# Layer 2's weights of a four-layer graph network from 16 concurrent 32x32 products and a table of block counts

## The reference, cut to what matters

```
def layer0(X, adj):   # mean of the neighbours, dense, relu, l2 norm
    deg = clip(sum(adj, 1) + 1, 1)
    z = concat([X, (adj @ X + X) / deg]) @ W + b
    out = relu(z); return out / max(norm(out), 1e-12)
def layer1(X, Wt=adj):
    h = tanh(concat([X, t]) @ W1 + b1)
    return h @ W2 + b2 + Wt @ (X @ B.T) - sum(Wt, 1) * (X @ B.T)
def layer2(X, adj):   # a neighbour weighs 1, 1/2, 1/4, ... from the last one of its row back
    rank = cumsum(adj != 0, 1); k = min(rank[:, -1:], 100)
    w = mask * where(pos > 0, 0.5 ** (k - pos), 0)       # pos = rank - (deg - k)
    return w @ (X @ weight) + bias
def layer3(x, adj):   # logmap(adj @ expmap(x)) @ kernel + bias
x = layernorm(x + layer_l(x))      # for l = 0, 1, 2, 3
```

## Time and profile before

| what | value |
|---|---|
| time, median of 3 runs | 167.0 us (166.5 to 167.3) |
| profiled execution | 167.19 us |
| its span | 165.3 us |
| PE busy | 123.7 us, 75% |
| DVE busy | 105.8 us, 64% |
| ACT busy | 70.6 us, 43% |
| POOL busy | 46.3 us, 28% |
| mean granted TensorE clock | 0.959 |

### The profile page before, as it was taken

One profiled execution on the slowest core, in us unless ns is written; L12 is line 12 of the kernel. 1 busy time (PEld: TensorE's weight loads), 2 busy tenths in 40 slices (PEclk: granted clock), 3 DMA queues, 4 the chain that ended last, 5 costly groups with the idle time before them and its releaser, 6 DMA issues.

```text
span 165.3 us, 2143 instructions
## 1 busy us (share of the span) xinstructions
PE 123.7 (75%) x760; PEld 67.6 (41%) x760; DVE 105.8 (64%) x235; ACT 70.6 (43%) x143; POOL 46.3 (28%) x54
## 2 busy tenths in 40 slices
PE   0000269996999999999997999989999899992000
PEld 0000159841444345346344667337447644572000
DVE  0164997999999999998961115500623888538861
ACT  0030215477567866715814576721113310257440
POOL 0000002412401241027931024400412552713290
PEclk9999999999999999999999999999999999998555
DMA  3999999999999940000000000000000000000006
GB/s 110 255 238 357 354 289 252 337 344 340 339 345 346 300 147 0 0 4 0 0 0 0 0 4 0 2 0 4 0 0 0 0 2 0 4 0 0 0 0 127
DMA packets 13946, 18.59 MB, mean 112 GB/s; under 512 B 5360, under 2 KB 5616, under 8 KB 13936
## 3 DMA queue, kind: packets, MB, share of 16 engines
q1 hardware_dynamic: 7728, 9.68, 20.6%
q10 hardware_dynamic: 6208, 8.78, 18.0%
HBM read 17.93 MB, written 0.52 MB: 112 GB/s over the span
## 4 chain that ended last, share of the span: by engine, by line
DVE 34%; PE 34%; DMA 13%; ACT 5%; POOL 4%; issue 4%; SPq 2%; POOLq 1%; DVEq 0%
PE psS L801 11%; DVE AT L556 8%; DMA stage<-adj 7%; DMA WT<-adj 7%; DVE AT L557 6%; PE psN L801 5%; PE psC L801 5%; POOL root L287 2%; PE psC L892 2%; PE psC L890 2%; POOL nroot L306 2%; DVE XP L562 2%; ACT WT L397 2%; DVE XP L561 1%; DVE u L579 1%
## 5 line engine op out<-in xcount | busy, mean ns | idle before, releaser
L397 ACT ACTIVATE WT<-psC 128x512 int16<-128x512 f32 x64 | 36.5, 597 | 13.3 <-PE psC L892 12.4
L801 PE MATMUL psS<-AT,XP 128*128 128x512 bf16 x112 | 29.9, 379 | 1.3 <-DVE XP L562 1.3
L287 POOL TENSOR_TENSOR root<-var,power 128x4 f32<-128x4 f32 (+1 forms) x16 | 18.7, 1172 | 36.5 <-DVE var L603 14.6
L892 PE MATMUL psC<-AT,cb 128*128 128x512 bf16 x64 | 24.2, 379 | 0.0
L890 PE MATMUL psC<-AT,cb 128*128 128x512 bf16 x56 | 21.4, 382 | 1.6 <-ACT WT L397 1.5
L556 DVE STREAM_TRANSPOSE AT<-stage 128x1024 bf16<-128x1024 bf16 x10 | 13.0, 1304 | 10.0 <-DMA stage<-adj 10.0
L801 PEld LDWEIGHTS psS<-AT,XP 128*128 128x128 f16 x112 | 10.4, 98 | 15.1 <-DVE XP L562 2.3
L854 PE MATMUL psH<-AT,cb 128*32 128x256 bf16 x32 | 1.7, 344 | 18.9 <-DVE AT L557 18.9
L300 POOL TENSOR_TENSOR XB<-X,weights 128x256 f32<-128x256 f32 x12 | 10.0, 843 | 18.4 <-DVE X L608 18.4
L557 DVE STREAM_TRANSPOSE AT<-stage 128x1024 bf16<-128x1024 bf16 x10 | 12.7, 1273 | 0.0
L391 ACT ACTIVATE stage<-psS 128x512 f32<-128x512 f32 x6 | 3.6, 596 | 17.6 <-PE psS L801 11.4
(11 more groups left out here) (156 smaller groups left out, 231.1 us busy)
## 6 DMA issues: line engine op xcount, KB each, us to landing
stage<-adj ACTq DMA_DIRECT2D x20, 256.0 KB, 11.3
stage<-adj SPq DMA_DIRECT2D x20, 256.0 KB, 13.4
WT<-adj ACTq DMA_DIRECT2D x12, 256.0 KB, 12.5
WT<-adj SPq DMA_DIRECT2D x12, 256.0 KB, 16.8
out<-X SPq DMA_DIRECT2D x6, 64.0 KB, 2.0
weights<-weights_packed SPq DMA_DIRECT2D x1, 353.5 KB, 17.2
X<-x SPq DMA_DIRECT2D x2, 128.0 KB, 6.8
X<-x ACTq DMA_DIRECT2D x2, 128.0 KB, 8.2
```

What stands on the lines that cost most here:

```text
L287: nc.gpsimd.tensor_tensor(root[:, e, 0:n], var[:, e, 0:n], power[:, 0:n, 0:NR], ALU.pow).then_inc(root_ready, 1)
L397: nc.scalar.activation(WT[:, e, chain_block(bank, k)], psC[bank][:], ACT.Relu).then_inc(chain_taken, 1)
L801: ins = nc.tensor.matmul(bank, XP[:, l % 2, c], matrix, start=(c == 0), stop=last)
L892: nc.tensor.matmul(acc, C("own"), AT[:, c, e], start=False, stop=True, skip_group_check=(k > 0)).then_inc(chain_ready, 1)
```

## The change

Layer 2's weights: `chain(i)` is now one step for four tiles of chunk i // 4, 16 steps in all. A step is 32 matmuls of 32x32 by 32x512: 16 from `base`, a constant, on `later`, and 16 from `own` on the matrix itself. In each set every one has its own 32 rows (q) and its own 32 columns (g) of the array; a row strip q writes its own PSUM bank. `later` is a table of counts, 17 rows per quarter, which a new matmul `spread` makes from `cnt` and ACT evicts (`take_spread`). No step needs the one before it, but the four banks of `psC` must have been evicted. ACT evicts two banks with one instruction (`take_chain(i, h)`). The tiles so made have their row quarters in another order, so layer 2's x parts are written to `ZP` and turned into that order by `turn` (16 matmuls of 128x32 per chunk, evicted by `take_turned`), before layer 2's sums.

Layer 1: two banks, `psN` and `psS`; chunks 0 and 1 first, then 2, then 3. `counts`, `spread` and `degrees` share `psX` with the transposed x and the hidden layer, from chunk 1 on. Layer 0's last chunk is counted and summed in three quarters of its columns after transposes 14, and the last quarter after transposes 15.

Other moves: centring of the weights on DVE goes from behind transposes 15 to ahead of transposes 4, and its DMA one block earlier in SP's queue; `residual(1, 0)` and `residual(1, 1)` on POOL go ahead, `diagonals(2)` and `(3)` and the roots are reordered; the constants grow from 801 to 1057 columns of 2 bytes.

```diff
-CCOLS = {"ident": P, "paired": P, "own": P, "past": P, "begin0": P, "begin1": P, "count": QD, "each": 1}
+NBLOCKS = 16
+CCOLS = {"ident": P, "paired": P, "own": QD, "base": NBLOCKS * QD, "spread": P, "count": NQ * QD, "each": 1}
...
+        ZP = Z[:].rearrange("p c f -> p (c f)").bitcast(F16).rearrange("p (c f) -> p c f", c=NB)
+
+        psC = psum("psC", [P, NQ, CW], F32)
+        psS = psum("psS", [P, CW], F32)
...
         def sum_bank(l, e):
-            return psS[0] if l == 0 else (psS[1], psN[1], psS[0], psC[0])[e]
+            if l == 0:
+                return psS[:]
+            return (psN[:], psS[:])[e % 2] if l == 1 else (psN[:], psC[:, 2], psC[:, 3], psS[:])[e]
...
         def dense_bank(l, e):
-            return psN[0] if l == 0 else (psN[0], psH)[e % 2] if l == 1 else (psN[0], psH, psX, psC[1])[e]
...
-            for m in range(1, NR):
+            for m in range(1, NR - 1):
                 load_lower(m)
             sp.dma_start(weights[:, first:WTOT], wpack[:, first:WTOT]).then_inc(weights_loaded, 16)
-            for m in range(NR, NB):
...
-            e = NE - 2
-            weigh(e)
-            l2_root(e)
-            weigh(e + 1)
-            residual(1, 0)
-            var_root(0, e)
-            diagonals(e)
-            residual(1, 1)
-            l2_root(e + 1)
-            diagonals(e + 1)
+                residual(1, e)
+            weigh(2)
+            diagonals(2)
+            l2_root(2)
+            weigh(3)
+            l2_root(3)
+            var_root(0, 2)
+            var_root(0, 3)
+            diagonals(3)
             residual(1, 2)
-            var_root(0, e + 1)
...
+            def take_spread(e):
+                act.wait_ge(spread_ready, e + 1)
+                nc.scalar.activation(natural(later[:, e % 2]), psX[:].rearrange("p (k h b) -> p k h b", h=2, b=QD),
+                                     ACT.Copy).then_inc(spread_taken, 1)
...
+            def take_chain(i, h):
+                act.wait_ge(chain_ready, PAIRS * i + h + 1)
+                e, m = i // NR, i % NR
+                tiles = slice(NQ * m + PAIRS * h, NQ * m + PAIRS * (h + 1))
+                nc.scalar.activation(WT[:, e, tiles], psC[:, PAIRS * h:PAIRS * (h + 1)], ACT.Relu
                                      ).then_inc(chain_taken, 1)
...
+            def take_turned(e):
+                act.wait_ge(turned, e + 1)
+                nc.scalar.activation(XP[:, 0, chunk(e)], turn_bank(e).rearrange("p (Q f) -> p Q f", Q=NQ),
+                                     ACT.Copy).then_inc(turned_taken, 1)
...
-            for m in range(2, 6):
+            for m in range(2, 4):
                 transposes(m)
             dve.wait_ge(weights_loaded, 16)
             nc.vector.scalar_tensor_tensor(W("h_bias"), W("w1t"), W("t"), W("h_bias"), ALU.mult, ALU.add
                                            ).then_inc(h_bias_ready, 1)
+            bundle = W(CENTRED[0], CENTRED[-1]).rearrange("p (k f) -> p k f", f=D)
+            step(nc.vector.tensor_reduce(wmean[:], bundle, AX_X, ALU.add))
+            nc.vector.scalar_tensor_tensor(bundle, wmean[:].unsqueeze(2).to_broadcast([P, len(CENTRED), D]), -1.0 / D,
+                                           bundle, ALU.mult, ALU.add).then_inc(centred, 1)
+            transposes(4)
+            transposes(5)
...
+            add_own_part(2)
             transposes(15)
             activate0(2)
-            bundle = W(CENTRED[0], CENTRED[-1]).rearrange("p (k f) -> p k f", f=D)
-            step(nc.vector.tensor_reduce(wmean[:], bundle, AX_X, ALU.add))
-            nc.vector.scalar_tensor_tensor(bundle, wmean[:].unsqueeze(2).to_broadcast([P, len(CENTRED), D]), -1.0 / D,
-                                           bundle, ALU.mult, ALU.add).then_inc(centred, 1)
             take_degrees(3)
+            add_own_part(3)
+            activate0(3)
             combine0(2)
-            activate0(3)
+            combine0(3)
             normalise(0, 2)
-            combine0(3)
             normalise(0, 3)
...
+            for e in range(NE):
+                add_residual(1, e)
+                if e == NE - 1:
+                    normalise(1, e - 1)
+                variance(1, e)
+                if e != NE - 2:
+                    normalise(1, e)
...
+                if c % NR == 0 and l == 2:
+                    pe.wait_ge(turned_taken, c // NR + 1)
+                if c % NR == 0 and l != 2:
...
+                if l == 1 and e == 0:
+                    pe.wait_ge(deg_taken, NE - 1)
+                if l == 1 and e == 2:
+                    pe.wait_ge(deg_taken, NE)
...
-                if e >= 1:
-                    pe.wait_ge(deg_taken, e)
+            def counts(e, cols=slice(0, CW)):
+                if e == NE - 1:
+                    pe.wait_ge(hid_taken, 2)
+                bank = psH if e == 0 else psX
                 for k in range(NR):
+                    one = C("count")[:, QD * k:QD * (k + 1)]
                     for g in range(NQ):
-                        ins = nc.tensor.matmul(psH[QD * g:QD * (g + 1)], C("count"), AT[:, NQ * g + k, e],
+                        ins = nc.tensor.matmul(bank[QD * g:QD * (g + 1), cols], one, AT[:, NQ * g + k, e, cols],
                                                start=(k == 0), stop=(k == NR - 1))
-                ins.then_inc(counts_ready, 1)
...
+            def spread(e):
+                pe.wait_ge(counts_taken, e + 1)
+                nc.tensor.matmul(psX[:], C("spread"), cnt[:].rearrange("p r Q b -> p (r Q b)"), start=True, stop=True
+                                 ).then_inc(spread_ready, 1)
...
             def degrees(e):
-                pe.wait_ge(counts_taken, e + 1)
+                pe.wait_ge(spread_taken, e + 1)
...
+                    pe.wait_ge(chain_taken, PAIRS * i)
+                if m == 0:
+                    pe.wait_ge(spread_taken, e + 1)
+                for q in range(NQ):
+                    rows = slice(QD * q, QD * (q + 1))
+                    for g in range(NQ):
+                        c = NQ * m + g
+                        nc.tensor.matmul(psC[QD * g:QD * (g + 1), q], C("base")[rows, QD * c:QD * (c + 1)],
+                                         later[rows, e % 2], start=True, stop=False)
+                for q in range(NQ):
+                    rows = slice(QD * q, QD * (q + 1))
+                    for g in range(NQ):
+                        ins = nc.tensor.matmul(psC[QD * g:QD * (g + 1), q], C("own")[rows], AT[rows, NQ * m + g, e],
+                                               start=False, stop=True)
+                    if q % PAIRS == PAIRS - 1:
+                        ins.then_inc(chain_ready, 1)
...
+            def turn(e):
+                pe.wait_ge(parts_ready, parts_count(2, e))
...
+                for q in range(NQ):
+                    for g in range(NQ):
+                        ins = nc.tensor.matmul(turn_bank(e)[QD * g:QD * (g + 1), P * q:P * (q + 1)],
+                                               C("ident")[:, QD * q:QD * (q + 1)], ZP[:, NQ * e + g],
+                                               start=True, stop=True)
+                ins.then_inc(turned, 1)
...
+            pe.wait_ge(transposed, 4)
+            counts(0, second)
+            sum_cols(0, 2, 4, spread_first)
+            degrees(0)
+            chain(0)
+            dense(0, 0)
+            chain(1)
+            chain(2)
+            for e in range(1, NE - 1):
+                pe.wait_ge(transposed, NR * (e + 1))
+                pe.wait_ge(deg_taken, e)
+                counts(e)
+                for c in range(NB):
+                    sum_block(0, e, c)
+                    if c == 1:
+                        chain(NR * e - 1)
+                    if c == 5:
+                        spread(e)
+                    if c == 10:
+                        degrees(e)
+                    if c == 11:
...
+                add_own(0, e)
+                sums(1, 0, range(e - 1, e))
+                dense(0, e)
+                if e == 1:
+                    chain(NR * e + 1)
+                    chain(NR * e + 2)
+                if e == 2:
+                    transpose_x(1, 0)
+                    hidden(0)
+                    transpose_x(1, 1)
+                    chain(NR * e + 1)
+                    hidden(1)
             e = NE - 1
+            pe.wait_ge(transposed, NB - 1)
+            counts(e, most)
+            pe.wait_ge(sum_taken, e)
+            sum_cols(e, 0, 3)
             pe.wait_ge(transposed, NB)
-            counts(e)
-            sums(0, e, range(0, 2))
+            counts(e, rest)
+            sum_cols(e, 3, 4)
+            chain(10)
+            spread(e)
...
+            dense(0, e)
+            sums(1, 1, range(0, 1))
+            chain(11)
+            sums(1, 1, range(1, 2))
+            chain(12)
+            transpose_x(1, 2)
+            sums(1, 0, range(2, 3))
+            hidden(2)
+            sums(1, 1, range(2, 3))
+            chain(13)
```

(23 more changed lines are left out.)

367 lines of the change are left out of this document (146 added, 221 removed).

## The result

The changed kernel takes 173.07 us (median of 4 runs, 172.62 to 173.45) against 167.0: 1.0366 times the time before, interval 1.0329 to 1.0402. The forecast was 169.5, slower by 1.5%; it is slower by 3.7%, inside the range. The profiled execution took 172.62 us with a span of 170.8; its mean granted clock was 0.920, that of the three others 0.902 to 0.910, so they had more of what follows; this execution was the shortest of the four.

What follows compares the result with a forecast made beforehand. No engine bounds it throughout: DVE the first half, PE from 87.6 to 120.9 us. Queue delays of 0.6 us on 167.0 give 167.6, clock falls add 1.9: 169.5 us, range 164.0 to 173.5.

Steps and rivals of the forecast that it cites:

- The clock: PE's clock falls in two idle stretches, before 57.8 and 88.5 us, costing 1.35 + 0.55 = 1.9 us.
- The walk: Queues followed up to layer 2's third group, clock held: 121.5 us against 120.9, +0.6.
- Prices: A chain step of 32 small matmuls takes 0.65 us against 1.73; a two-bank eviction 1.0, 0.91 between starts.
- Part 1: Up to the end of transposes 11: about +0.9 us, ending at 57.8 instead of 56.9.
- Part 2: Chunk 2 on PE, with two rounds through ACT: counts of chunk 3 at 72.8 us instead of 69.9.
- Part 3: Layer 0's end: DVE idle 5.6 us, PE 4 us, chunk 2's parts ready at 88.5 us.
- Part 4: PE from 88.5 us to layer 2's third group: 33.0 us instead of 33.3, to 121.5.
- Rival 1: The clock holds in both idle stretches before 57.8 and 88.5 us: 167.6 us, chance 0.24.
- Rival 2: Chunk 3's counts find `hid_taken` met under transposes 14, at 69 us; end 3.9 us earlier: 163.7 us, chance 0.25.
- Rivals 3 and 4: Chain steps held at about 1.0 us: 172.0 us, chance 0.07; row strips not overlapping: 175.9 us, chance 0.06.

Runs made afterwards that it cites:

- Experiment 1: The changed kernel with filler matmuls, results unused, in five places where TensorE idles (after chain steps 1, 2, 5, 6 and 12): 169.77 us, 1.0133.
- experiment 6: The changed kernel with 16 filler matmuls after chain step 12 alone: 170.55 us, 1.0192.
- Experiment 8: The kernel before, with layer 1's chunk 2 summed in one go instead of three of its four groups before the wait for layer 0: 170.89 us, 1.0167.
- degrees first: The change with its second round moved late, plus degrees of chunks 0 and 3 made ahead of `spread`: 164.39 us with fillers, 168.15 without.

## Why the prediction was right in kind and wrong in size

Two terms of the sum were too small, by about as much each. The clock was to cost 1.9 us and cost 3.1 by the profiled executions, 3.3 by the medians and 3.9 by the ratios. The walk with the clock held was to end 0.6 us behind before and ended 2.3 behind it. Experiment 1 has the clock held, so that the working can be compared with it, step by step, and the change with experiment 1.

| place | forecast, clock held | experiment 1 | the change |
|---|---|---|---|
| counts of chunk 2 begin | 57.8 | 58.48 | 58.67 |
| counts of chunk 3 begin | 72.8 | 74.00 | 75.46 |
| chunk 2's transposed x | 88.5 | 90.33 | 91.79 |
| layer 2's third group | 121.5 | 123.2 | 126.4 |

(123.2 is the turn at 122.04 plus the 1.14 us from turn to group in the change.)

**Prices: right.** A set of 16 products takes 0.225 us (103.57 to 103.79), a step some 0.58, against the 0.65 taken (it begins at 103.57; the first of the sixteen blocks behind it has no record, and stands 0.216 before the second, at about 104.15). Row strips do run side by side, as column strips do. The Trainium skill, page "TensorE: Matmul & The Clock Gate", section on packing small matmuls, gave an estimate of 0.65 by its 10.6 times; the trace is a tenth below it, with 0.58. A two-bank eviction takes 1.02, and two in a row 1.94 (1.0 and 0.91 between starts were taken). That ACT paces the steps now shows in PE's 6.0 us of waits for L402. The Trainium skill, page "TensorEngine Tiling (Array Packing)", section on the PSUM bottleneck, says that tiling leaves the eviction as it was, and the trace agrees: ACT is busy 70.8 us after 70.6.

**Part 1: +1.6 instead of +0.9, most of the excess from the clock at the start.** Chunk 0's degrees came at 34.47 us, after a wait of 0.98 on DVE: 1.3 behind the 33.19 of before, where 0.3 was taken. Rows of PE in the changed kernel, for the earlier trace rows:

```profile
22.69 3.62 PE L880 MATMUL psS<-AT,XP 128*128 128x256 bf16 x16
...
26.32 0.63 PE L852 MATMUL psX<-cb,XP 128*128 128x128 bf16 x4
...
27.91 0.39 PE L852 MATMUL psX<-cb,XP 128*128 128x128 bf16 x4
```

And in experiment 6's kernel, which is the same up to step 12:

```profile
26.08 0.39 PE L852 MATMUL psX<-cb,XP 128*128 128x128 bf16 x4
...
57.93 1.90 PE L872 MATMUL psX<-AT,cb 128*32 128x512 bf16 x16 [2.08 <-DVE AT L573]
```

PE began its blocks 0.37 later than at 22.32, the load's part (0.25 was taken). Four matmuls of 128x128 took 0.63 us at 26.32 and 0.39 at 27.91: the low level of the start, which was over at 25.6 before, reached to about 27 us here. From the blocks to the row at 27.91 it is 5.22 us, over the same work in before 4.64 (22.32 to 26.96), and behind it both take 3.4 to the counts. Experiment 1 has the same. In experiment 6's execution PE was at full clock by 26.08; chunk 0's degrees came at 33.84 without a wait, and chunk 2's counts began at 57.93, 0.1 from the forecast's 57.8. So the walk of DVE's queue was right. The 0.6 us is the length of the first low stretch, which differs between executions of the same instructions. DVE has no slack from there to the end of transposes 11, at 58.5 in the profiled execution.

**Part 2: mechanism right, 15.5 us instead of 15.0 with the clock held.** The wait on `hid_taken` is the one that ends last, and the two rounds took 3.0 and 3.7 us (68.77, 71.79, 75.46) for 2.9 and 3.6. The excess lies ahead of them: 8.8 us from the counts to the first round in experiment 1 for 8.5. The second fall, of 3.4 us, adds 1.3 (15.52 to 16.79), as its 1.35 in the forecast. In experiment 6's execution it lasted 6.8 us and added 1.8 (57.93 to 75.28); the mean clock of the change's three other executions, 0.902 to 0.910 for 0.920, is lower by some 3.4 to 6 us more at the low level (an estimate from the means and the span), and no trace shows where.

**Part 3: 16.3 us instead of 15.7**, in experiment 1 and in the change alike. DVE's idle time, 5.6 foreseen, is 7.1 in the one and 7.54 in the other, because the counts start later while DVE doesn't: it is through with chunk 2's part at 75.1. From the counts to the degrees it is 7.2 us (75.46 to 82.65) for 6.8, and DVE's chain behind them takes its 7.7 us (83.93 to 91.65). PE's idle time of 4 us is 4.17.

**Part 4: right.** 32.9 us in experiment 1 for 33.0. In the change it is 34.6: the third fall costs 1.75 (experiment 6), where 0.55 was counted.

**The clock: the failed term.** The step "each costs 3.7 / 2, less the waits that it covers, 1.35 + 0.55 = 1.9" had the length and the number wrong: three falls, of 6.8, 3.4 and 6.8 us, 17.1 in all, where two of 3.7 were foreseen. The one at 41.0, with waits of 2.03 and 2.13 us around step 2, I had not looked for; it costs little, since DVE's transposes set the pace there (chunk 2's counts begin 0.2 later than in experiment 1). The third is the mistake: twice as long as foreseen, it lasts on through layer 1's first blocks. Experiment 1 puts all three at 3.3 us, 1.4 over the forecast; by the ratios it is 3.9, 2.0 over.

**The walk: the other failed term, 1.7 us short**, 0.7 + 0.5 + 0.6 - 0.1 by the table. The 0.7 of part 1 is the late end of the low level at the start, and so a matter of the execution; the 1.0 of parts 2 and 3 is in small waits between queues that the walk put at nothing, for instance 0.3 ahead of the two rounds and 0.4 from the counts to the degrees. Beside its own before (167.47) experiment 1's median is 2.3 us longer, as by the rows (123.2 - 120.9). 2.0 for the clock and 1.7 for the walk make the 3.6 us between 169.5 and 173.07, within rounding.

**Rivals.** Rival 1, the clock holds: false. Rival 2, `hid_taken` met under transposes 14: not in the change; but its lever was found where I put it, in the two rounds. Moving one of them out gives 4.3 us by the medians and 3.1 by the profiles. Rivals 3 and 4 fall by the price of a step.

**Where did the gain in PE's work go?** The steps save what was promised, and 12.8 us of busy time are gone. They went from stretches in which PE now waits for DVE's transposes or for ACT; there they are idle time, and idle time brings the clock down. What was on PE's path, part 4, kept its length because layer 1's blocks were moved into it. Experiment 8 prices the order of chunk 2's 12 of these 20 blocks at 2.8 us on the kernel before. With the order mended and the gaps filled, a kernel with the cheap steps does beat before: 164.39, 2.0% under it. How much of that is the steps' isn't shown, since no run puts the old steps into that order.

**Open.** Why the low level at the start, and the second fall, last longer in one execution than in another isn't shown. Experiment 8's 2.8 us and the round's 4.3 can't be added, since each changes the other's clock; a version of the change that spreads chunk 2's sums over PE's gaps, as the kernel before does, was not tried.

## What to carry to other kernels

Work taken from an engine is worth something only where that engine ends the wait; elsewhere it turns into holes, and on TensorE holes have a price of their own, so after such a change read the granted clock beside the idle rows before reading anything else. Walk the queue of the engine that feeds the next stage (here the counts, behind a shared bank and two rounds through ACT), and move what isn't needed for it behind it: one moved round gave 3 to 4 us here. Where a gap can't be closed, throwaway matmuls into a free bank keep the clock (3.3 us here), and a shorter path should be tried with and without them: degrees first brought the next stage forward by 1.2 us both times, but gave 0.6 us of time without them and 2.0 with, as a fall behind it came or didn't.

## What the runs showed of the hardware

- The clock fell in stretches in which PE was never idle for more than 2.13 us at a time (39.74 to 42.52), though with little between: I had expected it after idle stretches of 3 or 4 us alone. In experiment 8 it fell 0.3 us after the end of a wait of 2.75 us (88.1, wait over at 87.78).
- A fall lasted 3.4, 6.8 or 10.2 us in the profiled executions, the second one 3.4 or 6.8 us in kernels whose instructions up to there are the same (the change, experiment 6), and went on while PE was busy throughout (3.40 of 3.40 us in experiment 8).
- The low level at the start was over by 26.08 us in experiment 6 and not yet at 26.32 in the change, whose instructions up to there are the same; PE's blocks had begun at 22.85 and at 22.69.
- Two sets of 16 products of 32x32 by 32x512 follow each other at 0.225 us, as one block of 128x512 follows another at 0.216; a third set adds 0.22.
- A product on DVE took 1.26 us beside POOL's 1.03 at 91.7 us in the changed kernel, 0.42 without: the new order on POOL moved it from chunk 2's way to chunk 3's.
